# Local attention layers: row sums, weights, transposes and value products of a unit issued one unit later

## The reference

```
q, k, v = split(x @ Wqkv)                 # 16 heads of 64
q = l2norm(q) * q_scale; k = l2norm(k) * k_scale      # t / max(norm, 1e-12)
q = q*cos*scale + rotate_half(q)*sin*scale            # and k with 1/scale
sim  = einsum("bhwie,bhwje->bhwij", q_w, k_w2) * 8    # own and previous window
attn = softmax(where(mask, -max, sim))
out  = einsum("bhwij,bhwje->bhwie", attn, v_w2) @ Wo
```

## Time and profile before

| what | value |
|---|---|
| median of three runs | 5334.38 us (5327.61 to 5336.43) |
| profiled execution, its own time | 5326.38 us |
| its span, first to last instruction | 5324.4 us |
| mean granted clock of PE, of full speed | 0.892 |
| busy over the span: PE, DVE, ACT, POOL | 85%, 54%, 48%, 52% |
| local stage, six layers | about 595 to 2391 us of the span |

### The profile page before, as it was taken

The page is one execution under the profiler, slowest core; times in us unless marked ns, Lnnn a source line. Parts: engine busy times, 40 slices in busy tenths (PEclk is TensorE's granted clock), DMA queues, the critical chain, the costliest instruction groups (busy, mean ns, idle before and its releaser), DMA issues. The chain is left out here.

```text
span 5324.4 us, 68492 instructions
## 1 busy us (share of the span) xinstructions
PE 4501.7 (85%) x21823; PEld 2217.4 (42%) x21823; DVE 2850.4 (54%) x3426; ACT 2555.3 (48%) x4400; POOL 2778.0 (52%) x1598
## 2 busy tenths in 40 slices
PE   6988676777777676777986999999999999999983
PEld 2333343443434343442333454444444454545431
DVE  3676463746556463744655555555555555555505
ACT  1544463635446363631452555555555555555540
POOL 0000352635445352520001888888888888888880
PEclk6877798988989898985786999999999999999996
DMA  0000000000000000000001000000000000000000
GB/s 17 3 2 0 33 1 22 1 22 1 17 6 13 10 1 21 1 1 11 1 1 30 2 1 3 3 3 3 3 3 3 3 1 4 2 4 1 1 0 8
DMA packets 18027, 34.97 MB, mean 7 GB/s; under 512 B 3418, under 2 KB 12250, under 8 KB 16746
## 3 DMA queue, kind: packets, MB, share of 16 engines
q1 hardware_dynamic: 17642, 30.22, 1.8%
HBM read 29.69 MB, written 0.52 MB: 6 GB/s over the span
## 5 line engine op out<-in xcount | busy, mean ns | idle before, releaser
L1169 POOL TENSOR_TENSOR xat_p_sum<-xat_p_sum,xat_p_full 128x1024 f32<-128x1024 f32 x768 | 1836.1, 2391 | 227.3 <-ACT xat_p_full L1119 190.9
L1211 DVE TENSOR_REDUCE xat_part<-xat_ring 128x2 f32<-128x1024 f32 (+1 forms) x832 | 951.7, 1181 | 559.1 <-PE xat_ring L989 556.5
L1119 ACT ACTIVATE xat_p_full<-xat_sc 128x512 f32<-128x512 f32 (+1 forms) x1632 | 870.5, 594 | 727.1 <-PE xat_sc L1029 690.8
L1015 PE MATMUL xat_acc<-xat_p_full,xat_v 128*64 128x512 f32 (+1 forms) x3264 | 792.0, 605 | 0.0
L1028 PE MATMUL xat_sc<-xat_q_hh,xat_k_hl 128*128 128x512 f32 (+1 forms) x1632 | 776.1, 476 | 15.4 <-ACT xat_p_full L1119 14.0
L1029 PE MATMUL xat_sc<-xat_q_lm,xat_k_h 128*128 128x512 f32 (+1 forms) x1632 | 645.3, 395 | 0.0
L1706 POOL TENSOR_TENSOR loc_weights_n<-loc_probs,loc_rinv 128x512 f32<-128x512 f32 (+1 forms) x384 | 303.4, 811 | 458.8 <-DVE loc_rinv L1802 307.6
L1690 POOL TENSOR_TENSOR loc_sind<-loc_qk,loc_tab 128x512 f32<-128x512 f32 x192 | 238.9, 1266 | 456.6 <-DVE loc_ss L1746 456.6
L1485 PE MATMUL loc_pr<-loc_w_qkv,loc_xs 128*128 128x512 f32 x576 | 362.6, 763 | 101.1 <-DVE loc_cosd L1753 55.7
L1028 PEld LDWEIGHTS xat_sc<-xat_q_hh,xat_k_hl 128*128 128x128 f32 (+1 forms) x1632 | 303.0, 186 | 301.3 <-issue 155.4
L987 PE MATMUL xat_ring<-xat_k_hl,xat_q_hh 64*128 64x512 f32 (+1 forms) x832 | 332.3, 456 | 29.5 <-DVE xat_part L1211 20.4
(11 more groups left out here) (393 smaller groups left out, 7184.6 us busy)
## 6 DMA issues: line engine op xcount, KB each, us to landing
loc_w_qkv<-in_L_ffn_w SPq DMA_DIRECT2D x6, 1536.0 KB, 7.2
loc_w_o<-in_L_ffn_wo SPq DMA_DIRECT2D x6, 512.0 KB, 3.2
xat_ctxT<-in_ctxT SPq DMA_DIRECT2D x12, 256.0 KB, 2.7
xat_w_qk<-in_L_xattn_wqk SPq DMA_DIRECT2D x16, 128.0 KB, 2.0
loc_w<-in_L_ffn_w SPq DMA_DIRECT2D x6, 341.0 KB, 3.1
loc_w<-in_L_ffn_w SPq DMA_DIRECT2D x6, 192.0 KB, 2.4
loc_rope<-in_rope SPq DMA_DIRECT2D x1, 1024.0 KB
xat_w_o<-in_L_xattn_wo SPq DMA_DIRECT2D x16, 64.0 KB, 1.9
```

The source lines that it names most:

```text
L1015: last = pe.matmul(acc[h * GROUP:(h + 1) * GROUP, :], v[0:size, t, e * GROUP:(e + 1) * GROUP], p_full[0:size, (e * NT + t) % RING, cols(h) ...
L1119: act.activation(p_full[0:size, at_.buffer(t), cols(h)], sc[0:size, n % 3, :], ACT.Exp, scale=GROUP ** -0.5).then_inc(S["exp_done"], 1)
L1169: pool.tensor_tensor(p_sum[:, e, :], first_in, p_full[:, at_.buffer(t), :], ALU.add)\
L1211: ins = dve.tensor_reduce(part[:, 2 * t:2 * t + 2, c], ring[:, b, :, 0:chunks[c][1]], AX.X, ALU.max)
```

## The change

R is issued at the next even step, behind the following unit's M, so R(x) stands with M(x+1). W follows at step 2x+3 instead of 2x+1, T at 2x+5 instead of 2x+3, and O at 2x+7 instead of 2x+4. On PE an odd step now reads S(x), O(x-4), T(x-3), so that O uses weights transposed one odd step earlier, and even steps hold no work of units. On ACT att(x-4) stands ahead of pT(x-3) in the same step. E and M keep their steps. The bound of the norms becomes a `scalar_tensor_tensor` with the same tensor as both inputs. Buffers and semaphores stay as they are; the only DMAs of the layers, on SP's queue, are not moved.

```
@@ order of the slots of tr
-            if step % 2 and 0 <= step - 3 < STEPS:
+            if step % 2 and 0 <= step - 5 < STEPS:
                 for kind in "pe":
-                    tr_at[kind, (step - 3) // 2] = len(tr_at)
+                    tr_at[kind, (step - 5) // 2] = len(tr_at)
@@ tensor, units(step), behind S
-                    x = (step - 3) // 2
-                    if step % 2 and 0 <= x < UNITS:
-                        pe.wait_ge(S["p_done"], i * UNITS + (x + 1))
...
-                    x = (step - 4) // 2
-                    if step % 2 == 0 and 0 <= x < UNITS:
+                    x = (step - 7) // 2
+                    if step % 2 and 0 <= x < UNITS:
                         t, u = divmod(x, UN)
                         pe.wait_ge(S["tr_free"], i * (TR * NTOK) + (tr_at["e", x] + 1))
...
                         last.then_inc(S["o_ps"], 1)
+                    x = (step - 5) // 2
+                    if step % 2 and 0 <= x < UNITS:
+                        pe.wait_ge(S["p_done"], i * UNITS + (x + 1))
...
@@ scalar, units(step), behind E
-                    x = (step - 3) // 2
+                    x = (step - 7) // 2
+                    if step % 2 and 0 <= x < UNITS:
+                        t, u = divmod(x, UN)
+                        act.wait_ge(S["o_ps"], i * UNITS + (x + 1))
+                        act.activation(att[:, 2 * u:2 * u + 2, t * P:(t + 1) * P],
+                                       out_ps[:, :, 0:P],
+                                       ACT.Copy).then_inc(S["o_free"], 1)
+                    x = (step - 5) // 2
                     if step % 2 and 0 <= x < UNITS:
                         n = tr_at["p", x]
...
-                    x = (step - 5) // 2
-                    if step % 2 and 0 <= x < UNITS:
-                        t, u = divmod(x, UN)
-                        act.wait_ge(S["o_ps"], i * UNITS + (x + 1))
...
@@ gpsimd, units(step)
-                    x = (step - 1) // 2
+                    x = (step - 3) // 2
                     if step % 2 and 0 <= x < UNITS:
                         pool.wait_ge(S["inv_done"], i * UNITS + (x + 1))
@@ vector, prepare, p == 3
-                        dve.tensor_scalar(ss[:], ss[:], 1e-12, None, ALU.max).then_inc(S["bound_done"], 1)
+                        dve.scalar_tensor_tensor(out=ss[:], in0=ss[:], scalar=1e-12, in1=ss[:], op0=ALU.max,
+                                                 op1=ALU.max).then_inc(S["bound_done"], 1)
@@ vector, units(step), behind M
-                    x = (step - 1) // 2
-                    if step % 2 and 0 <= x < UNITS:
+                    x = (step - 2) // 2
+                    if step % 2 == 0 and 0 <= x < UNITS:
                         dve.wait_ge(S["exp_done"], i * UNITS + (x + 1))
```

More of the change, by code:

```diff
@@ L1555, in units @@
                         last.then_inc(S["o_ps"], 1)
+                    x = (step - 5) // 2
+                    if step % 2 and 0 <= x < UNITS:
+                        pe.wait_ge(S["p_done"], i * UNITS + (x + 1))
+                        n = tr_at["p", x]
+                        pe.wait_ge(S["tr_free"], i * (TR * NTOK) + (n - 1))
+                        for c in range(4):
+                            last = pe.transpose(tr[:, n % 2, c * P:(c + 1) * P], weights_n[:, x % 4, c * P:(c + 1) * P],
+                                                g.ident[:])
+                        last.then_inc(S["tr_ps"], 1)
+                        n = tr_at["e", x]
+                        pe.wait_ge(S["tr_free"], i * (TR * NTOK) + (n - 1))
+                        pe.transpose(tr[:, n % 2, 0:P], weights_n[:, x % 4, 4 * P:4 * SPAN], g.ident[:])\
+                          .then_inc(S["tr_ps"], 1)
                 attention(units, prepare)
@@ L1642, in units @@
                         act.activation(pT2[:, x % 2, :], tr[:, n % 2, 0:P], ACT.Copy).then_inc(S["tr_free"], 1)
-                    x = (step - 5) // 2
-                    if step % 2 and 0 <= x < UNITS:
-                        t, u = divmod(x, UN)
-                        act.wait_ge(S["o_ps"], i * UNITS + (x + 1))
-                        act.activation(att[:, 2 * u:2 * u + 2, t * P:(t + 1) * P],
-                                       out_ps[:, :, 0:P],
-                                       ACT.Copy).then_inc(S["o_free"], 1)
                 attention(units, prepare)
```

## The result

| | before | after |
|---|---|---|
| median of four runs | 5335.41 us (5327.61 to 5338.06) | 5476.36 us (5463.26 to 5492.06) |
| profiled execution, its own time | 5326.38 us | 5492.06 us |
| its span | 5324.4 us | 5489.0 us |
| mean granted clock of PE in it | 0.892 | 0.860 |

The ratio is 1.0279 with an interval of 1.0256 to 1.0303: the change costs 141 us, three times the 46 that I forecast, and more than the upper end of my range. 10.6 of them lie ahead of the first layer, whose S(0) starts at 645.77 instead of 635.14 us, in work that the change does not touch; from S(0) to S(28) the six layers add up to 1269.7 instead of 1117.9 us, which is 151.8 more; the last 3 us lie elsewhere.

What follows compares the result with a forecast made beforehand. A loop through PE, ACT and DVE was taken as the bound, no single engine. Tiles 1 to 5 at 28.52 against 27.15 us, plus layer ends, gave 7.65 us a layer, 46 in six: 5380 us, range 5318 to 5442.

Steps and rivals of the forecast that it cites:

- The loop: Tiles 1 to 5: O ahead of T and Q lengthens the full-clock loop from 25.54 to 26.91 us, 1.37 more.
- The clock: PE in tiles 1 to 5: at least one fall to the lower clock, priced at 1.6 us, 28.5 us a tile.
- my bound of 30.1: Upper bound of a tile in us, with two clock falls, at X and K and at S and Q; chance 0.12.
- a single fall: Tiles 1 to 5: one clock fall a tile, or between one and two, giving 5380 us; chance 0.60.
- Tile 0 and tile 6: Ends of each local layer: tile 0 unchanged (from -1.0 to +1.6 us), tile 6 longer by 1.3 us.
- Tile 7: Last tile of each local layer: about 21.5 us against 22.05, taken as -0.5 us.
- The bound: Norms' bound on DVE: the two-tensor form still waits for POOL's addition, near 1.1 us; no gain, at most 6 us.
- the lock of which the prediction spoke: SBUF port pair shared by VectorE and GpSimd: exclusive lock, so the bound's new form waits as the old did.
- The sum: Per local layer, tiles 1 to 5 plus tiles 0, 6 and 7: 7.65 us longer; six layers 46 us.
- The rival that the clock stays up: Tiles 1 to 5: no clock fall, 1.6 us a tile won and 1.37 lost, 5320 us; chance 0.09.
- the rival that the change does what it says: ACT and DVE have slack, so two 1.11 us waits a tile vanish: 18.7 us a layer, 112 us, 5222; chance 0.08.

Runs made afterwards that it cites:

- run 2: The changed kernel with unread products filling PE's gaps to size, two ahead of X and three between the transposes of k and q: 5319.35 us, 0.999 of before.
- run 10: The kernel before with one unread product of 384 columns ahead of X, nothing moved: 5302.58 us, 0.9959 of before.
- run 4: The changed kernel with only the gap between the transposes of k and q filled by unread products: 5363.49 us, 1.0066 of before.
- run 8: The changed kernel with O at step 2x+8, behind the next T, and both gaps filled with unread products: 5242.33 us, 0.9847 of before.
- run 3: The changed kernel with only the gap ahead of X filled by unread products: 5418.85 us, 1.0172 of before.
- run 7: The changed kernel with O at step 2x+8, behind the next unit's T, and no gaps filled: 5424.23 us, 1.0164 of before.

## Why the prediction was wrong in size

**The loop: right.** 26.91 us worked out, 26.92 measured at full clock in run 2, and in its tile from 693.47 us on the three parts take 10.66, 7.48 and 8.77 us against 10.66, 7.47 and 8.78; the waits of V, S, X, K and the transposes are within 0.25 us of those foretold. O in front of T and Q does lengthen the loop, by 1.37 us against 25.54.

**The clock: the term that failed,** as the prediction put it: "At least one fall a tile is likely. I price it at the 1.6 us measured". In 23 of the 30 tiles 1 to 5 there are two, in the other seven one that lasts as long as both. In the tile shown the two cost 12.81 + 9.16 + 9.41 - 26.91 = 4.47 us: 1.69 in the part with K, as priced, and 2.78 in the two others. So this tile takes 31.38 us, where two falls at 1.6 gave my bound of 30.1. The new stretch lasts 6.8 us, twice that at K, and holds almost nothing but PE work on the loop (transposes, S, O, T), as the timeline above shows. The error was to price a second fall by the one kind that tiles 1 to 5 of the trace of before had: 1.6 us is what K loses. That trace held a longer one elsewhere: tile 6 of layer 4, with some 13.6 us at 0.50 behind the same 1.94 us ahead of X, takes 26.05 us where the tile 6 of the other layers takes 24.2 to 24.4.

**How many falls.** I gave a single fall the larger chance because the gaps of 1.1 us in the trace of before were followed by none. The gap that mattered is the 2.18 us for `kT`, which my own text had at 2.2, longer than the 1.94 behind which the clock had fallen. By the row that I had, two falls were the likeliest. The premise was too narrow as well: in run 10 the clock falls behind waits of at most 1.11 us, and in run 4 it often holds behind 1.66. What decides whether a wait is followed by a fall stays open.

The Trainium skill, page "TensorE: Matmul & The Clock Gate", section "A second HAM failure mode: psum-queue depth-cycling", tells of a kernel whose PE idles briefly but often between groups of products, so that the clock swings between its two levels and the throughput suffers. The trace after agrees: 0.50 at 735, 1.00 at 742, 0.50 at 756, 1.00 at 759 us.

**Tile 0 and tile 6.** 0 and +1.3 forecast, +1.71 and +3.80 measured. At full clock (run 2) tile 6 takes 25.15 us, 0.5 more than my 24.66; the other 2.9 are the lower clock (0.75, against 0.93 in the earlier trace rows). Tile 0 was 25.53 in run 2 and 27.73 after.

**Tile 7:** -0.5 forecast, 0.07 measured to the start of the output product (22.24 against 843.32 - 821.15 = 22.17). The clock was 0.95 there. In run 2, at clock 1.00, it is 21.59 us (847.87 - 826.28), 0.58 under before: the forecast holds at full clock, and the lower clock takes the gain back.

**The bound: right.** In the trace after it takes 1.18 us and ends at 753.10, POOL's addition at 753.05:

```profile
751.92 1.18 DVE L1774 SCALAR_TENSOR_TENSOR loc_ss<-loc_ss 128x32 f32<-128x32 f32 x1 [1.41 <-ACT loc_ss L1601]
...
756.14 3.17 DVE L1759 TENSOR_TENSOR loc_cosd<-loc_cosd,loc_ss 128x1024 f32<-128x1024 f32 x2
```

```profile
750.70 2.35 POOL L1695 TENSOR_TENSOR loc_cosd<-loc_cosd,loc_sind 128x1024 f32<-128x1024 f32 x1
...
756.38 3.19 POOL L1706 TENSOR_TENSOR loc_weights_n<-loc_probs,loc_rinv 128x512 f32<-128x512 f32 x2 [1.98 <-DVE loc_rinv L1803]
```

The W below it is stretched by DVE's scaling. The Trainium skill, page "SBUF — State Buffer", section "SBUF: two separate sides", has the lock of which the prediction spoke; these rows agree with it.

**The sum.** For layer 1 I had 0 + 6.85 + 1.3 - 0.5 = 7.65 us; it is 1.71 + 20.83 + 3.80 + 0.07 = 26.4. In run 2, with the clock at 1.00 in all but tile 0 (0.94), the same four are -0.49 - 1.18 + 0.92 - 0.58 = -1.33 us. That doesn't make the order free, since the kernel before has a fall in most of its tiles: of the 4.17 us that a tile gets longer, 1.38 are the order (26.92 against 25.54 at full clock) and 2.79 the clock (31.32 - 26.92 = 4.40 after, 27.15 - 25.54 = 1.61 before). The rival that the clock stays up had 5320 us, and run 2 gives 5319.35; as shares of the kernel before of their sessions these are 0.9973 and 0.999, so that they meet within a microsecond is luck. And the rival that the change does what it says needs O behind T and Q and a clock that stays up: then it is 84 us, in run 8, not 112 (its 18.7 us a layer should have been 18.4, 7 x 2.2 + 3).

## What to carry to other kernels

When PE waits in a loop that several engines share, work out the loop first, and then, as a term of its own, where the gaps will lie and what PE work stands behind each: in these tiles a fall cost somewhat under half of its length (1.6 us for some 3.4 and 2.6 for some 6.8 in run 3, 4.1 for some 10 in the trace after, each against 26.92), so price each fall by its own length and the work in it, and not by the one in the trace. How long it will be, and whether it comes at all, these runs did not let me foretell; filling the gaps settled it. An operation with ready inputs still delays everything behind it in its queue; move it behind the operations that start the next link of the loop, not only behind those it waits for. And where a gap can't be closed by real work, products that nobody reads, cut to a little less than the gap, can be worth more than the reordering itself, as here.

## What the runs showed of the hardware that was not expected

Gaps of 2.18 us (the trace after) and 1.86 us (run 7) in PE's work, with PE busy ahead of and behind them, were followed in the tiles shown by some 6.8 us at clock 0.50; 1.53 and 1.78 us of filling kept the clock at 1.00 in 26 of the 30 tiles 1 to 5 of run 2. But a gap's length tells neither whether a fall follows nor how long it lasts: behind some 2.18 us it lasted 3.4, 6.8 or 10 us in run 3, and in run 10 half of the tiles kept the clock and half did not, with the same instructions and waits of at most 1.11 us.

POOL's W next to DVE's scaling of k and q, both now in one go of 3.17 us, takes 3.19 us instead of 1.40 (2.21 before). It cost the loop nothing: in run 2 W takes 3.19 us beside the same neighbours, and the tile of 26.92 us leaves no room for it.
